# Routed experts in 256-row tiles with a transposed first layer, in a gated cross-attention and mixture-of-experts block

## The reference

```python
x = x + tanh(g_xattn) * cross_attention(layernorm(x), ctx)   # 16 heads of 64, q and k normalised per head
h = layernorm(x)
probs = softmax(h  Wg)                       # 8 experts
vals, idx = top_k(probs, 2)
weights = vals / (sum(vals) + 1e-9)
for each chosen expert e of a token:          # W1[e] 128 x 512, W2[e] 512 x 128
    y[e] = silu(h  W1[e] + b1[e])  W2[e] + b2[e]
out = sum(weights[e] * y[e]) + 0.1 * (silu(h  Ws1 + bs1)  Ws2 + bs2)
x = x + tanh(g_ffn) * out
```

## Time and profile before

| | |
|---|---|
| runs, us | 870.76, 868.55, 868.52; median 868.55 |
| profiled execution, its span (first to last instruction), us | 835.4 |
| its own time beside the span | not recorded on its page; the median of the runs stands 33.15 us above the span |
| TensorE matmul busy, us | 716.7 (86%) |
| VectorE, ScalarE, GpSimd busy, us | 559.3, 437.2, 474.0 |
| mean granted TensorE clock | 0.950 of full speed |
| row stage, first transpose of rows to the last copy of an answer, us from the span's start | 606.5 to 808.7 |

### The profile page before, as it was taken

How to read it: one execution, slowest core, us unless ns; L and a number is a source line. 1 busy time by engine, 2 the same in 40 slices (tenths; PEclk the granted TensorE clock), 3 DMA queues, 4 the chain that set the end, 5 groups by cost and what they waited for, 6 DMA issues and landing times.

```text
span 835.4 us, 22819 instructions
## 1 busy us (share of the span) xinstructions
PE 716.7 (86%) x7888; PEld 608.6 (73%) x7889; DVE 559.3 (67%) x1340; ACT 437.2 (52%) x856; POOL 474.0 (57%) x494
## 2 busy tenths in 40 slices
PE   1679999999999999999999839988089999999950
PEld 1568888888888888888888738888068788887840
DVE  5647888888888888888888756888423344343326
ACT  2546666666676666666667515554023333333324
POOL 3554676767676767676767453777613333333320
PEclk9999999999999999999999977999579999999995
DMA  6151000000000000000000010111211111111119
GB/s 208 23 189 43 5 7 3 6 3 6 3 6 3 6 3 6 3 6 3 6 0 2 2 27 7 55 47 55 71 42 53 50 46 50 50 48 47 50 45 280
DMA packets 41714, 32.74 MB, mean 39 GB/s; under 512 B 6016, under 2 KB 36048, under 8 KB 41680
## 3 DMA queue, kind: packets, MB, share of 16 engines
q1 hardware_dynamic: 33392, 18.27, 7.9%
q0 software_dynamic: 4672, 9.04, 3.1%
q10 hardware_dynamic: 3616, 4.99, 2.1%
HBM read 20.15 MB, written 12.13 MB: 39 GB/s over the span
## 4 chain that ended last, share of the span: by engine, by line
PE 71%; DVE 8%; ACT 8%; issue 6%; DMA 3%; POOL 2%; ACTq 1%; SPq 0%; DVEq 0%; POOLq 0%
PE ps L1122 8%; PE ps L1006 8%; PE ps L956 7%; PE ps L927 7%; PE ps L910 5%; PE ps L912 4%; PE ps L911 4%; ACT spo L408 4%; PE ps L1019 4%; PE ps L990 4%; PE ps L1127 4%; PE ps L1057 2%; PE ps L1104 2%; PE ps L1107 2%; PE ps L1105 2%
## 5 line engine op out<-in xcount | busy, mean ns | idle before, releaser
L531 POOL TENSOR_TENSOR rstd<-var_eps,expo 128x16 f32<-128x16 f32 x64 | 186.3, 2911 | 5.0
L594 POOL DMA_INDIRECT results<-spo,xs_ix x72 | 69.6, 967 | 138.3 <-ACT spo L472 135.2
L384 ACT ACTIVATE qk_T<-ps,lnw 128x512 f32<-128x512 f32 x128 | 96.4, 784 | 62.4 <-PE ps L927 62.2
L888 DVE COPY qk_T<-ps 128x512 f32<-128x512 f32 x72 | 49.8, 692 | 73.0 <-PE ps L1127 73.0
L910 PE MATMUL ps<-w_hi,xc_hi 128*128 128x512 f32 x192 | 92.1, 480 | 0.9 <-DVE prob L686 0.9
L707 DVE TENSOR_TENSOR wide<-ps,rstd 128x512 f32<-128x512 f32 x128 | 84.6, 683 | 7.2 <-POOL rstd L531 7.2
L927 PE MATMUL ps<-ident,wide 128*128 128x128 f32 x512 | 74.7, 280 | 12.6 <-DVE xc_lo L623 12.1
L460 ACT ACTIVATE xs_hi<-ps 128x128 fp32r<-128x128 f32 x72 | 20.0, 277 | 119.4 <-PE ps L1112 119.4
L1122 PE MATMUL ps<-w_sb,qk_T 128*128 x576 | 81.3, 284 | 0.0
L557 POOL DMA_INDIRECT routed<-w_raw,slot x64 | 63.9, 998 | 30.1 <-issue 18.9
L673 DVE TENSOR_REDUCE ss<-wide 128x16 f32<-128x1024 f32 x64 | 77.5, 1210 | 4.5 <-ACT wide L392 3.3
(11 more groups left out here) (182 smaller groups left out, 1612.4 us busy)
## 6 DMA issues: line engine op xcount, KB each, us to landing
v_sb<-routed SPq DMA_DIRECT2D x72, 64.5 KB, 1.8
c_in<-in_ctx SPq DMA_DIRECT2D x32, 64.0 KB, 1.8
w_raw<-in_L_ffn_W ACTq DMA_DIRECT2D x1, 2048.0 KB, 9.0
wide<-results SPq DMA_DIRECT2D x8, 256.0 KB, 4.8
w_raw<-results SPq DMA_DIRECT2D x8, 256.0 KB, 4.9
out_x<-x_res SPq DMA_DIRECT2D x8, 256.0 KB, 4.1
results<-spo,xs_ix POOLq DMA_INDIRECT x72, 2.5
routed<-w_raw,slot POOLq DMA_INDIRECT x64, 2.3
```

The costliest lines, as they stand in the source:

```text
L384: nc.scalar.activation(qk_T[:, n, 4 * j:4 * j + 4, :].rearrange("p a n -> p (a n)"), ps[6 + j][:, :], ACT.Identity, bias=lnw[:, 2 * n + 1: ...
L531: nc.gpsimd.tensor_tensor(rstd[:, n, :], var_eps[:, n, :], expo[:, n, :], ALU.pow).then_inc(rstd_ready, 1)
```

## The change

The row stage and what feeds it are rewritten.

- Tiles have 256 rows (`RT`), and there are 39 of them (2 x 4096 / 256 + 7). All 39 are written out; there is no loop.
- The first layer is made transposed. The expert's weights, in pieces of 128 x 128, are the stationary operand and the 256 rows the moving one: per tile 4 pieces x 3 products. The result has hidden units on the partitions, so the transposes L1127 and the copies L888 are gone.
- The expert's first-layer weights are first copied by VectorE from `w1_hi` and `w1_lo` to the fixed place `w1_now` (two buffers, two copies of 128 x 512 a tile), in `row_weights`.
- b1 comes in as the bias of the Silu, four activations of 128 x 256 a tile. b2 comes in when VectorE copies the answer from PSUM to `yb` (an addition). The bias matmuls L1104 and L1119, the bias preparation on GpSimd and the tile `rows3` are gone. Two DMAs load b1 by hidden unit and b2 broadcast to all partitions.
- A tile is loaded by one DMA of 256 rows and scattered by two indirect DMAs.
- VectorE, ScalarE and TensorE each read the tile's expert into a register.
- The pads are 256 rows, in two tiles, so GpSimd clears two.

The core of the diff:

```diff
-REGION = TOKENS + P
-SPARE = 8
-NT = 72
+RT = 256
+SUB = RT // P
+REGION = TOKENS + RT
+NT = 2 * TOKENS // RT + E - 1
+SPARE = E - 1
...
+        PADS = (E + SPARE) * SUB
+        pad_i = sb("pad_i", [P, PADS], I32)
+        pad = spo[:, 0:E * SUB * ROW].rearrange("p (e a n) -> p e a n", e=E, a=SUB)
+        pad_s = v_sb[:, :, :].rearrange("p a n -> p (a n)")[:, 0:SPARE * SUB * ROW].rearrange("p (k n) -> p k n", n=ROW)
+        xs_in = v_sb[:, :, :].rearrange("p a n -> p (a n)")[:, 0:4 * SUB * ROW].rearrange("p (k a n) -> p k a n", k=4, a=SUB)
+        xs_hi = sb("xs_hi", [P, 2, RT], F32R)
+        xs_lo = sb("xs_lo", [P, 2, RT], F32R)
+        xs_ix = sb("xs_ix", [P, 4, SUB], I32)
+        w1_now = sb("w1_now", [P, 2, 2, FF], F32R)
+        hT = qk_T[:, :, :, :].rearrange("p a b n -> p (a b n)")[:, 0:2 * CH * RT].rearrange("p (u c n) -> p u c n", u=2, c=CH)
+        yb = o_T[:, :, :, :].rearrange("p a b n -> p (a b n)")[:, 0:4 * SUB * D].rearrange("p (k a n) -> p k a n", k=4, a=SUB)
...
-            def step(n, q, k, u):
-                if is_row_tile(k + 2):
-                    row = sp.value_load(tile_of_sched(1, n + 2), min_val=0, max_val=E * REGION + SPARE * P - P)
-                    if k + 2 >= 4:
-                        sp.wait_ge(r_t, n - 1)
-                        sp.wait_ge(r_ix, n - 1)
-                    b4 = (q + 2) % 4
-                    sp.dma_start(xs_in[:, b4, :], routed[bass.ds(row, P), :]).then_inc(r_in[b4], 16)
-
-            row_steps(sp, step)
-
+            for n in range(NT):
+                b4, landed = r_slot(n)
+                row = sp.value_load(sched_i[0:1, 1, n:n + 1], min_val=0, max_val=E * REGION + (SPARE - 1) * RT)
+                if n >= 4:
+                    sp.wait_ge(r_t, n - 3)
+                    sp.wait_ge(r_ix, n - 3)
+                sp.dma_start(xs_in[:, b4, :, :], routed[bass.ds(row, RT), :].rearrange("(a p) n -> p a n", p=P)).then_inc(r_in[b4], 16)
...
+            def row_hi(n):
+                sc.wait_ge(r_t, n + 1)
+                if n >= 2:
+                    sc.wait_ge(r_h, 2 * (n - 1))
+                nc.scalar.activation(xs_hi[:, n % 2, :], ps[6 + n % 2][:, 0:RT], ACT.Copy).then_inc(r_hi, 1)
+
+            def row_silu(n):
+                expert = sc.value_load(sched_i[0:1, 0, n:n + 1], min_val=0, max_val=E - 1)
+                if n >= 2:
+                    sc.wait_ge(r_y, n - 1)
+                for c in range(CH):
+                    if c % 2 == 0:
+                        sc.wait_ge(r_h, 2 * n + c // 2 + 1)
+                    nc.scalar.activation(hT[:, n % 2, c, :], ps[2 * (n % 2) + c // 2][:, (c % 2) * RT:(c % 2 + 1) * RT], ACT.Silu,
+                                         bias=b1_cols[:, bass.ds(expert * CH + c, 1)]).then_inc(r_act, 1)
+
+            sc.wait_ge(sched_ready, 1)
+            sc.wait_ge(bias_in, 32)
+            row_hi(0)
+            row_hi(1)
+            row_silu(0)
+            for n in range(NT):
+                if n + 1 < NT:
+                    row_silu(n + 1)
+                if n + 2 < NT:
+                    row_hi(n + 2)
...
             gp_.wait_ge(y_done, TILES)
-            nc.gpsimd.memset(pad[:, :, :], 0.0).then_inc(pad_ready, 1)
-            gp_.wait_ge(pad_ready, 1)
-            nc.gpsimd.tensor_copy(pad[:, :, D].bitcast(I32), i32s[:, 200:200 + 2 * E]).then_inc(pad_ready, 1)
-
-            n1 = E * FF // P
-            gp_.dma_start(b_raw[:, 0:n1], b1.rearrange("e f -> (e f)").rearrange("(p n) -> p n", p=P)).then_inc(bias_in, 16)
-            gp_.dma_start(b_raw[:, n1:BC], b2.rearrange("e f -> (e f)").rearrange("(p n) -> p n", p=P)).then_inc(bias_in, 16)
-            nc.gpsimd.memset(b1_parts[:, :, :], 0.0).then_inc(bias_prep, 1)
-            nc.gpsimd.memset(b2_parts[:, :, :], 0.0).then_inc(bias_prep, 1)
-            gp_.wait_ge(bias_in, 32)
-            done = 2
-            for n in range(3):
-                if n > 0:
-                    gp_.wait_ge(bias_prep, done)
-                    nc.gpsimd.tensor_tensor(b_raw[:, :], b_raw[:, :], b_cols[:, n - 1, :], ALU.subtract).then_inc(bias_prep, 1)
-                    done += 1
-                    gp_.wait_ge(bias_prep, done)
-                nc.gpsimd.tensor_copy(b_cols[:, n, :], b_raw[:, :]).then_inc(bias_prep, 1)
-                done += 1
-            gp_.wait_ge(bias_prep, done)
-            for lo, hi, dram in ((0, n1, bias1), (n1, BC, bias2)):
-                gp_.dma_start(dram.rearrange("a (p n) -> p a n", p=P), b_cols[:, :, lo:hi]).then_inc(bias_in, 16)
-            gp_.wait_ge(bias_in, 64)
-            for n in range(3):
-                at = slice(32 * n, 32 * n + 1)
-                gp_.dma_start(b1_parts[at, :, :].rearrange("p e n -> p (e n)"), bias1[n:n + 1, :]).then_inc(bias_ready, 16)
-                gp_.dma_start(b2_parts[at, :, :].rearrange("p e n -> p (e n)"), bias2[n:n + 1, :]).then_inc(bias_ready, 16)
+            nc.gpsimd.memset(pad, 0.0).then_inc(pad_zero, 1)
+            nc.gpsimd.memset(pad_s, 0.0).then_inc(pad_zero, 1)
+            gp_.wait_ge(pad_zero, 2)
+            nc.gpsimd.tensor_copy(pad[:, :, :, D].bitcast(I32), pad_i[:, 0:E * SUB].rearrange("p (e a) -> p e a", e=E)).then_inc(pad_ready, 1)
+            nc.gpsimd.tensor_copy(pad_s[:, :, D].bitcast(I32), pad_i[:, E * SUB:PADS]).then_inc(pad_ready, 1)
+            gp_.dma_start(b1_cols[:, :], b1).then_inc(bias_in, 16)
+            gp_.dma_start(b2_all[:, :, :].rearrange("p e n -> p (e n)"), b2.rearrange("(a e) n -> a (e n)", a=1).partition_broadcast(P).rearrange("p a n -> p (a n)")).then_inc(bias_in, 16)
             groups(gp_, group)
...
+            for n in range(NT):
+                b4, _ = r_slot(n)
+                gp_.wait_ge(r_yb, n + 1)
+                for a in range(SUB):
+                    gp_.indirect_dma_start(out=results[:, :], out_offset=bass.IndirectOffsetOnAxis(ap=xs_ix[:, b4, a:a + 1], axis=0),
+                                           in_=yb[:, b4, a, :], in_offset=None).then_inc(r_sent[b4], 16)
...
+            def row_lo(n):
+                ve.wait_ge(r_hi, n + 1)
+                nc.vector.tensor_tensor(xs_lo[:, n % 2, :], ps[6 + n % 2][:, 0:RT], xs_hi[:, n % 2, :].bitcast(F32), ALU.subtract).then_inc(r_lo, 1)
+
+            def row_index(n):
+                b4, landed = r_slot(n)
+                ve.wait_ge(r_in[b4], landed)
+                if n >= 4:
+                    ve.wait_ge(r_sent[b4], 16 * SUB * (n // 4))
+                nc.vector.tensor_copy(xs_ix[:, b4, :], xs_in[:, b4, :, D].bitcast(I32)).then_inc(r_ix, 1)
+
+            def row_weights(n):
+                expert = ve.value_load(sched_i[0:1, 0, n:n + 1], min_val=0, max_val=E - 1)
+                if n >= 2:
+                    ve.wait_ge(r_h, 2 * (n - 1))
+                for u, w in enumerate((w1_hi, w1_lo)):
+                    nc.vector.tensor_copy(w1_now[:, n % 2, u, :], w[:, bass.ds(expert, 1), :].rearrange("p a n -> p (a n)")).then_inc(r_w, 1)
+                return expert
+
+            ve.wait_ge(bias_in, 32)
+            experts = [row_weights(0), row_weights(1)]
+            row_lo(0)
+            row_lo(1)
+            for n in range(NT):
+                b4, _ = r_slot(n)
+                expert = experts[n % 2]
+                if n + 2 < NT:
+                    row_lo(n + 2)
+                row_index(n)
+                ve.wait_ge(r_y, n + 1)
+                nc.vector.tensor_tensor(yb[:, b4, :, :], ps[4 + n % 2][:, 0:SUB * D].rearrange("p (a n) -> p a n", a=SUB),
+                                        b2_all[:, bass.ds(expert, 1), :].to_broadcast([P, SUB, D]), ALU.add).then_inc(r_yb, 1)
+                if n + 2 < NT:
+                    experts[n % 2] = row_weights(n + 2)
...
+            def row_transpose(n):
+                b4, landed = r_slot(n)
+                pe.wait_ge(r_in[b4], landed)
+                if n >= 2:
+                    pe.wait_ge(r_lo, n - 1)
+                for a in range(SUB):
+                    last_ = nc.tensor.transpose(ps[6 + n % 2][:, a * P:(a + 1) * P], xs_in[:, b4, a, 0:D], ident[:, :])
+                last_.then_inc(r_t, 1)
+
+            def row_hidden(n):
+                pe.wait_ge(r_lo, n + 1)
+                pe.wait_ge(r_w, 2 * n + 2)
+                if n >= 2:
+                    pe.wait_ge(r_act, CH * (n - 1))
+                for c in range(CH):
+                    h = ps[2 * (n % 2) + c // 2][:, (c % 2) * RT:(c % 2 + 1) * RT]
+                    w_hi_c, w_lo_c = (w1_now[:, n % 2, u, c * P:(c + 1) * P] for u in range(2))
+                    nc.tensor.matmul(h, w_hi_c, xs_hi[:, n % 2, :], start=True, stop=False)
+                    nc.tensor.matmul(h, w_hi_c, xs_lo[:, n % 2, :], start=False, stop=False)
+                    last_ = nc.tensor.matmul(h, w_lo_c, xs_hi[:, n % 2, :], start=False, stop=True)
+                    if c % 2 == 1:
+                        last_.then_inc(r_h, 1)
+
+            def row_out(n):
```

(84 more changed lines are left out.)

102 lines of the change are left out of this document (15 added, 87 removed).

## The result

The changed kernel takes 891.4 us (median of 4 runs, 883.7 to 894.0), where the kernel before takes 868.8 beside it: ratio 1.0236, 95% interval 1.0209 to 1.0264. It is slower, by 22.6 us; I had forecast +14.9 and 883. The profiled execution took 893.99 us, with a span of 892.2.

What follows compares the result with a forecast made beforehand. TensorE bound the row stage before, a wait for weight copies after. Last answer +13.6 (groups' 4.2 gain included), second scatter +1.3: +14.9 on span 835.4 gives 850.3, plus 33.15 makes 883 us; range 861 to 910.

Steps and rivals of the forecast that it cites:

- The new wait: Row stage: each next first layer waits for VectorE's weight copies behind the second layer; rounds of 5.62 us against 3.68 of work.
- Rival 1: Row stage: shorter stall, register load hidden, addition's address free, 256-column product bound by weight load; rounds 5.0, 861 us; chance 0.15.
- Rival 2: Row stage: the stall is hidden and the change does what it removes; rounds 3.7, about 814 us; chance 0.04.
- The clock: Row stage: TensorE's clock, taken as full in the summed 36 rounds of 5.62 us; its fall was left to a rival.
- my own signs of being wrong: Row stage: first layer following at once, 256-column products spaced 0.17, granted clock below 1, or VectorE late by `xs_lo`.
- Rival 3: Row stage: TensorE's clock falls in the stall, 2.7 us more a round; a quarter of rounds +25, all +100; chance 0.2.
- the likeliest case: Whole kernel: the forecast itself, row-stage rounds of 5.2 to 6.1 us, 868 to 900 us; chance 0.55.
- First transpose to third first layer: Filling of the row stage, from its first transpose to the first layer of tile 2: 11.1 us.
- From the last first layer to the end of the last addition: End of the row stage, from `row_hidden(38)` to the last answer: 6.1 us.
- The groups: Ahead of the groups: fewer GpSimd clears free VectorE's small addition, so first logits and scatters come 4.2 us earlier.
- The second scatter: End of the kernel: a tile needs a second scatter, +1.3 us.
- The 33.15 us "around the span": Whole kernel: the median time was taken to lie 33.15 us above the profiled span, so this was added to 850.3.

Runs made afterwards that it cites:

- the kernel with the weights first: The changed kernel with VectorE's weight copies for tile n+2 put first in round n instead of last: 775.4 us, ratio 0.9258 to the kernel before.
- The filled gap: The changed kernel with ten more TensorE products of 256 columns after each second layer, results unread: 847.9 us, ratio 1.0099 to the kernel before.
- the third chip: The changed kernel and the kernel before, both unaltered, profiled once each on another chip: 861.4 and 838.8 us.

## Why the prediction was right, and where its sizes were off

**The new wait** was the step that carried the forecast, and it is right in place and order. By its own times, counted from the first start of a first layer: ScalarE's copy forecast to end near 3.0, measured 2.98 (706.69); `xs_lo` 3.45, measured 3.44; the addition at 3.97, measured 3.81; copies done at 5.48, measured 5.35; the round 5.62, measured 5.45 at full clock. The difference is there when the second layer's last matmul ends, at 3.66 and not at 3.85: TensorE's 256-column product is spaced 0.118 (I took 0.128), and the 16 matmuls took 1.95, not 2.09. (In the list of times 3.97 + 0.71 is 4.68, not 4.70; that is 0.7 us in 36 rounds.) Rival 1 (5.0) needed a hidden register load, and it stands in the trace, with 0.35 (forecast 0.3); moved ahead of the wait it gave 0.33 a round. Rival 2 is what the kernel with the weights first made of it: 3.52, where I had counted 3.68.

**The clock** is the mis-sized term, and "the granted clock below 1 in the stage" stood among my own signs of being wrong. The sum had none of it: 36 x 5.62 = 202.3 us. Measured were 209.8 in the first profile: 36 x 5.44 = 195.8 and some 14 from rounds at half clock, 8 of 36 rounds at 1.6 each and three of 5.8. So two errors stood against each other, 6.5 us too much for the rounds and 14 too little for the clock, and that the difference came out within 8 us is in part luck. Rival 3 had the mechanism, with a quarter of the rounds and 2.7 us each, +25: the count fits (8 and 11 in two profiles, 4 in the fastest run), the price does not, since a long round is at half clock only in part (the first products of the one shown ran at full clock). So the likeliest case and rival 3 were one case with a smaller price, and the sum missed the 6 to 18 us (4 to 11 rounds at 1.6) that it had set beside itself with 0.2. The Trainium skill, "TensorE: Matmul & The Clock Gate", section "Why this matters for your kernels", names idle gaps between bursts of matmuls as what drops the clock to half. The filled gap agrees in kind: without the idle time the granted clock stayed at 1.00. The price of a gap as short as 1.77 us came from the runs alone.

**The other terms.** First transpose to third first layer: 11.1 forecast, 649.6 - 638.84 = 10.8. From the last first layer to the end of the last addition: 6.1 forecast, 865.15 - 859.4 = 5.75. The stage from its first transpose to there: 226.3, forecast 219.5, before 202.1. The groups: -3.8, forecast -4.2. The mechanism of the clears was confirmed and my picture of it, one slow addition, was too narrow. The second scatter: forecast +1.3. Its last scatter starts at 867.43, 2.28 behind the end of the last addition, before 0.75 behind the last copy (809.40): +1.5. Stage +24.2, groups -3.8, scatter +1.5: +21.9 against the 22.6 measured, if the pauses cost both kernels the same. On the third chip neither profile has pauses, and the spans differ by 22.6 too (837.1 and 859.6): the stage +28.9 with its eleven long rounds, the last scatter +1.5, the stage's start -7.6, the rest -0.2. Of the -7.6 again 3.8 are the clears, and 2.1 an attention that ended sooner in this one execution. Another 1.2 are the scatters of the groups, of which I had said that their time stays: from the first to the last pass 82.1 to 82.3 us in the three profiles of the kernel before and 80.9 to 81.1 in the changed ones without pauses. Why is not known.

**The 33.15 us "around the span"** was a wrong attribution. About 1.8 us lie outside a span (893.99 - 892.2, 838.15 - 836.4). The profile shown was from an execution without the pauses. They come in kernels of both kinds, so far as times tell: the changed kernel took 891 us in the first measurement and 857 and 861 in later ones, the kernel before 869 and 838. So they fell out of the difference, and adding them as a constant gave an absolute figure, 883, that is near to 891 by luck. The difference is what to judge by: +14.9 forecast, +22.6 and +18.2 measured.

## What to carry to other kernels

In a program written per engine, read the list of the engine that serves the critical one, and ask of each instruction that feeds the next tile what it stands behind; here two copies behind an unrelated wait cost 1.9 us a round, more than the 1.74 us of matmuls that the change removed (5.26 - 3.52), and moving them up gave some 80 us (ratio 0.9258 in place of 1.0219 to the kernel before). A load of a register just ahead of the instruction that uses it is part of the chain: make it ahead of the wait. And a stall of TensorE that comes back every round can be priced twice, once for its length and once for the clock: here 1.77 us a round were, 1.44 were in one kernel, and 1.45 were not in the other.

## What the runs showed of the hardware

- The granted clock fell to its lower level, 1.2 GHz, in the row stage of kernels in which TensorE idled 1.44 to 2.47 us once a round, and was at 2.4 GHz throughout where it idled 0.58 or not at all. With 1.44 and 1.45 us it fell in one kernel and not in the other; with 1.77 the same kernel had 4, 8 and 11 long rounds in three profiles. In the kernel before it fell at 479.6 behind a gap of 1.49 us and stayed up behind gaps of 1.51 and 1.48 (up to 562.24 and 582.41).
- A load of a register from SBUF, with its check and the address, takes VectorE 0.6 to 0.7 us, of which it can do half while its last instruction still runs.
- A product of 128x128 weights with 256 columns is spaced 0.118 us, hardly more than the 0.11 of one with 8 columns.
- GpSimd's clears stop a multiplication of VectorE between SBUF tiles of 128x128 until they end (0.28 becomes 4.79 us); its scatters don't stop a copy of 128x512 (0.43 us).
- The pauses of some 5 us a group, in several engines at a time, stand in the first profile of the changed kernel alone; in none of the ten later profiles, on three chips, did they come back. What they wait for the trace does not name, and no run here settles it.

Weights read from `w1_hi` and `w1_lo` directly as the stationary operand, without copies, were not tried.
